# Fused block (GRU, state-space mixer, attention and experts): the 16-tap convolution of the mixer moved onto TensorE, with shifted copies made by transfers

## What is computed

```python
zxbcdt = x @ W_in                                   # x: the GRU's output, (32, 128, 128)
xBC = zxbcdt[..., D_INNER:D_INNER + CONV_DIM]       # 384 channels
kernel = conv_w.T[:, None, :]                       # conv_w: (384, 16)
xBC = jax.lax.conv_general_dilated(xBC, kernel, window_strides=(1,), padding=[(D_CONV - 1, 0)],
    dimension_numbers=('NWC', 'WIO', 'NWC'), feature_group_count=CONV_DIM) + conv_b
xBC = jax.nn.silu(xBC)
xs, Bm, Cm = ...                                    # 256, 64 and 64 channels of xBC
# scan over time: h = h * dA + dt * x * B;  y = h . C;  gated by silu(z), normalised, @ W_out
```

## Time and profile before

| | |
|---|---|
| median of 3 runs | 2272.22 us (2269.23 to 2278.43) |
| the profiled execution | 2269.55 us, its span 2267.7 us |
| busy share of the span | PE 89%, DVE 75%, ACT 44%, POOL 20% |
| chain that ended last | PE 47%, DVE 30%, ACT 9%, issue 8% |
| GRU and loads | 0 to 264.7 us |
| mixer with convolution | 264.7 to about 630 us |
| end of the mixer, then the later layers | to 2267.7 us |

### The profile page before, as it was taken

How to read it: one execution, slowest core, us unless ns; L and a number is a source line. 1 busy time by engine, 2 the same in 40 slices (tenths; PEclk the granted TensorE clock), 3 DMA queues, 4 the chain that set the end, 5 groups by cost and what they waited for, 6 DMA issues and landing times.

```text
span 2267.7 us, 62486 instructions
## 1 busy us (share of the span) xinstructions
PE 2011.8 (89%) x25711; PEld 1278.0 (56%) x25787; DVE 1698.1 (75%) x3792; ACT 1008.1 (44%) x2835; POOL 459.9 (20%) x794
## 2 busy tenths in 40 slices
PE   7888888998886898898799999985999789999998
PEld 5555534444453444343576677763666556677776
DVE  3443489999965888777888888844999668888887
ACT  2333245666553221221555555542544445555555
POOL 2211000000000434336012222243432111121200
PEclk8999699999978999999999999996999999999999
DMA  2000000000010000000311111106553211111111
GB/s 61 3 4 4 2 1 1 1 1 1 1 38 15 0 1 1 1 1 1 112 48 44 44 44 44 39 4 130 107 108 73 65 40 44 39 44 44 44 57 38
DMA packets 76038, 76.61 MB, mean 34 GB/s; under 512 B 15756, under 2 KB 57060, under 8 KB 74180
## 3 DMA queue, kind: packets, MB, share of 16 engines
q1 hardware_dynamic: 71848, 70.11, 12.3%
q10 hardware_dynamic: 3904, 2.49, 0.4%
HBM read 60.09 MB, written 11.82 MB: 32 GB/s over the span
## 4 chain that ended last, share of the span: by engine, by line
PE 47%; DVE 30%; ACT 9%; issue 8%; DMA 1%; POOL 1%; ACTq 1%; SPq 1%; another core or an unknown queue 1%; DVEq 0%; POOLq 0%
PE B L85 46%; DVE work L107 6%; DVE work L2117 4%; DVE hr L2081 3%; DVE work L2125 3%; ACT work L103 2%; ACT hr L103 2%; ACT ltc L103 2%; DVE work L1496 1%; ACT catt L103 1%; DVE gzh L107 1%; ACT ghh L103 1%; DVE work L1040 1%; ACTq L2404 1%; DVE grh L107 1%
## 5 line engine op out<-in xcount | busy, mean ns | idle before, releaser
L85 PE MATMUL B<-gr,wres 128*128 128x512 f32 x1248 | 354.5, 412 | 16.4 <-DVE work L2125 10.1
L103 ACT ACTIVATE work<-B 128x512 f32<-128x512 f32 (+7 forms) x468 | 240.1, 529 | 145.4 <-PE B L85 90.2
L2167 POOL COPY G<-lh 128x32 f32<-128x32 f32 x256 | 148.2, 579 | 680.0 <-DVE lh L107 680.0
L85 PE MATMUL B<-work 128*128 128x128 bf16 (+3 forms) x1408 | 260.3, 312 | 28.0 <-ACT work L103 7.0
L85 PEld LDWEIGHTS B<-gr,wres 128*128 128x128 f32 x1248 | 215.1, 189 | 83.7 <-DVE work L2125 27.4
L103 ACT ACTIVATE hr<-work 128x512 fp32r<-128x512 f32 x272 | 173.0, 636 | 147.0 <-DVE work L2125 77.5
L85 PEld LDWEIGHTS B<-work 128*128 128x128 bf16 (+2 forms) x1408 | 141.4, 127 | 139.1 <-issue 79.9
L2081 DVE TENSOR_TENSOR hr<-work,hr 128x512 fp32r<-128x512 f32 x272 | 186.5, 686 | 8.1 <-ACT hr L103 6.6
L2117 DVE TENSOR_TENSOR work<-work 128x512 f32<-128x512 f32 x256 | 178.9, 699 | 16.1 <-ACT work L103 8.9
L107 DVE SCALAR_TENSOR_TENSOR work<-work,cw 128x512 f32<-128x512 f32 x240 | 179.2, 747 | 5.9
L85 PE MATMUL B<-hr,wres 128*128 128x512 f32 x624 | 178.0, 394 | 1.0 <-DVE hr L2081 1.0
(11 more groups left out here) (262 smaller groups left out, 3777.8 us busy)
## 6 DMA issues: line engine op xcount, KB each, us to landing
work<-wdr SPq DMA_DIRECT2D x128, 256.0 KB, 3.1
scr<-catt SPq DMA_DIRECT2D x144, 64.0 KB, 2.8
work<-scr SPq DMA_DIRECT2D x16, 384.0 KB
work<-scr SPq DMA_DIRECT2D x16, 192.0 KB
catt<-in_L_ffn_ew SPq DMA_DIRECT2D x24, 128.0 KB, 2.2
work<-scr SPq DMA_DIRECT2D x16, 128.0 KB
out<-work SPq DMA_DIRECT2D x32, 64.0 KB, 2.2
work<-in_x ACTq DMA_DIRECT2D x2, 512.0 KB, 5.3
```

What stands on the lines that cost most here:

```text
L85: return e.matmul(out, lhsT, rhs, start=start, stop=stop, skip_group_check=True)
L103: return e.activation(out, in_, func, bias=bias, scale=scale)
L2167: e.tensor_copy(self.G[:, :, t], self.lh[:, t % 4, :]).then_inc(*inc("l.pool", "h", li, t))
```

## The change

All 16 taps go to PE. For that the 128 rows of the array no longer hold 128 channels, but 32 channels four times, each copy shifted by four more steps; the four column strips of the array (32 outputs each) take the four sets of 32 channels. In one wave, the four strips each do four taps for their 32 channels; four waves with the start moved by one column do all 16. A piece is so 4 waves of 4 matmuls of 32 x 512.

- The shifted copies are XR (two buffers in `spare`, which grows to 5120 columns): 4 row groups g, 4 sets of channels j. Each (g, j) is one transfer inside SBUF of 32 partitions x 4 x 131 words, from XP. SP issues these 16 transfers for each piece in the new `conv_sp` (L798), once `conv.x` of the piece is there and `conv.taps` of the piece two before has freed the buffer. PE waits for all 16 (`conv.r`).
- DVE's ten stt and `conv.acc` go. ACT's tanh waits for its own `conv.b`, and XP is freed by the transfers.
- The input product of piece n + 1 is now issued ahead of the taps of piece n, and the first one a turn before the loop; ACT's copy moves with it.
- The tap matrices (48 of 128 x 32 instead of 18 of 128 x 128) are made by three tensor_tensor on POOL after steps 60, 64 and 68 of the GRU, from the stacked identity `id32` (one reduce on DVE) and `cwp` (four more loads of 32 x 12 x 4 words on SP). DVE's 18 tensor_scalar go.

The diff, cut to its core:

```diff
-NT = 6
+NT = 16
...
-        for c in range(3):
-            for k in range(NT):
-                ts(e, self.tap[:, c * NT + k, :], self.ident[:], self.cw[:, c, k:k + 1], ALU.mult)
-                yield
+        red(e, self.id32[:], self.ident[:].rearrange("p (j m) -> p m j", j=4), ALU.add)
...
     def conv_pe(self, e):
+        e.wait_ge(*at("conv.tap"))
+        inputs(0)
+        yield
+        for n in range(24):
+            if n < 23:
+                inputs(n + 1)
+            yield
+            e.wait_ge(*at(f"conv.r{n % 2}", n))
+            if n:
+                e.wait_ge(*at("conv.b", n - 1))
+            for m in range(NT // 4):
+                for j in range(4):
+                    last = mm(e, BT[32 * j:32 * j + 32, :], self.tap[:, NT // 4 * (4 * (n % 3) + j) + m, :],
+                              self.XR[n % 2][:, 4 * j:4 * j + 4, m:m + 128], m == 0, m == NT // 4 - 1)
+                if m < 2:
+                    yield
+            last.then_inc(*inc("conv.taps", n))
+            yield
...
     def conv_dve(self, e):
-                e.wait_ge(*at("conv.b", n))
-                for k in range(NT, 16):
-                    stt(e, acc, X[:, :, 1 + k:129 + k], self.cw[:, c, k:k + 1], acc, ALU.mult, ALU.add)
...
+    def conv_sp(self, e):
+        for n in range(24):
+            e.wait_ge(*self.at("conv.x", n))
+            if n >= 2:
+                e.wait_ge(*self.at("conv.taps", n - 2))
+            for g in range(4):
+                for j in range(4):
+                    e.dma_start(self.XR[n % 2][32 * g:32 * g + 32, 4 * j:4 * j + 4, :],
+                                self.XP[n % 3][32 * j:32 * j + 32, :, 1 + NT // 4 * g:128 + NT // 4 * (g + 1)])
```

More of the change, by code:

```diff
@@ L171, in __init__ @@
         self.bank = [ctx.enter_context(nc.psum_tensor(f"B{i}", [128, 512], F32)) for i in range(8)]
-        with nc.sbuf_tensor("spare", [128, 3072], F32) as self.spare:
+        with nc.sbuf_tensor("spare", [128, 5120], F32) as self.spare:
             pass
@@ L255, in sync @@
         self.load_sp(e)
+        self.conv_sp(e)
         self.cprep_sp(e)
@@ L516, in gru_pool @@
                 next(rest, None)
+            if t in (60, 64, 68):
+                x = t - 60
+                e.wait_ge(*at("mprep.dve", "id32"))
+                e.tensor_tensor(self.tap[:, x * NT // 4:(x + 4) * NT // 4, :], bc(self.id32[:], 1, NT),
+                                bc(self.cwp[:, x:x + 4, :].rearrange("p x m -> p (x m)"), 2, 32), ALU.mult).then_inc(
+                    *inc("conv.tap"))
             yield
@@ L536, in lay_mamba @@
         self.h0T = sb("h0T", [64, 256])
-        self.tap = self.area([self.work, 74 * 256 - 3 * NT * 128], [128, 3 * NT, 128])
+        self.cwp = sb("cwp", [128, 12, NT // 4])
+        self.id32 = sb("id32", [128, 32])
+        self.tap = self.area([self.work, 74 * 256 - 96 * NT], [128, 3 * NT, 32])
+        w = [self.spare, 0]
+        self.XR = [self.area(w, [128, 16, 127 + NT // 4]) for _ in range(2)]
         w = [self.work, 0]
@@ L570, in mprep_load @@
             pairs.append((self.cb[:, c:c + 1], col(I["L0_attn_conv_b"][c * 128:c * 128 + 128])))
+        taps = I["L0_attn_conv_w"].rearrange("(x r) k -> r x k", r=32)
+        for g in range(4):
+            pairs.append((self.cwp[32 * g:32 * g + 32, :, :], taps[:, :, NT // 4 * g:NT // 4 * (g + 1)]))
         for d, s in pairs:
@@ L604, in mprep_dve @@
             yield
-        for c in range(3):
-            for k in range(NT):
-                if c + k == 0:
-                    e.wait_ge(*at("xt", 7))
-                ts(e, self.tap[:, c * NT + k, :], self.ident[:], self.cw[:, c, k:k + 1], ALU.mult)
-                yield
+        red(e, self.id32[:], self.ident[:].rearrange("p (j m) -> p m j", j=4), ALU.add).then_inc(*inc("mprep.dve", "id32"))
+        for _ in range(6):
+            yield
         e.wait_ge(*at("mprep.act", "A"))
@@ L672, in conv_pe, with inputs @@
         e.wait_ge(*at("mprep.dve", "A"))
[L673 to L680, removed]
-                yield
[L682 to L693, removed]
+        e.wait_ge(*at("conv.tap"))
+        def inputs(n):
+            if n:
+                e.wait_ge(*at("conv.x", n - 1))
+            mm(e, BI[:], self.win[:, 256 + n % 3 * 128:384 + n % 3 * 128], flat(self.G, UNITS[n // 3]), True, True).then_inc(
+                *inc("conv.in", n))
+        inputs(0)
[5 more added lines that the diff above has]
+            e.wait_ge(*at(f"conv.r{n % 2}", n))
+            if n:
+                e.wait_ge(*at("conv.b", n - 1))
[6 more added lines that the diff above has]
+            last.then_inc(*inc("conv.taps", n))
+            yield
+            if n % 3 == 2:
+                yield
     def conv_act(self, e):
@@ L707, in tanh @@
         def tanh(n):
-            e.wait_ge(*at("conv.acc", n))
+            e.wait_ge(*at("conv.b", n))
             if n >= 2:
@@ L712, in conv_act, with inputs @@
         e.wait_ge(*at("conv.pad"))
+        def inputs(n):
+            e.wait_ge(*at("conv.in", n))
+            if n >= 3:
+                e.wait_ge(*at(f"conv.r{(n - 3) % 2}", n - 3))
+            act(e, self.XP[n % 3][:, :, 16:144], BI[:].rearrange("p (b t) -> p b t", b=4), ACT.Copy).then_inc(
+                *inc("conv.x", n))
+        inputs(0)
+        yield
         n = 0
@@ L750, in silu @@
                 stt(e, cv[0:64, c, :], th[0:64, :], 1.0, cv[0:64, c, :], ALU.add, ALU.mult).then_inc(*inc("conv.silu", n))
-        for _ in range(4):
+        for _ in range(5):
             yield
@@ L755, in conv_dve @@
             for c in range(3):
-                X, acc = self.XP[n % 3], self.cvb[u % 4][:, c, :].rearrange("p (b t) -> p b t", b=4)
                 yield
@@ L759, in conv_dve @@
                     silu(n - 1)
-                e.wait_ge(*at("conv.b", n))
-                for k in range(NT, 16):
[L762 to L767, removed]
+                for _ in range(3):
+                    yield
                 n += 1
@@ L771, in conv_dve @@
         yield
+    def conv_sp(self, e):
[3 more added lines that the diff above has]
+                e.wait_ge(*self.at("conv.taps", n - 2))
+            else:
+                e.wait_ge(*self.at("conv.pad"))
+            for g in range(4):
+                for j in range(4):
+                    e.dma_start(self.XR[n % 2][32 * g:32 * g + 32, 4 * j:4 * j + 4, :],
+                                self.XP[n % 3][32 * j:32 * j + 32, :, 1 + NT // 4 * g:128 + NT // 4 * (g + 1)]).then_inc(*self.dma(f"conv.r{n % 2}", n))
     def conv_pool(self, e):
```

## The result

The changed kernel takes 2290.24 us (median of 5 runs, 2285.11 to 2293.76), the kernel before 2272.73 in the same comparison: a ratio of 1.0077, 95% interval 1.006 to 1.0093. It is slower by 0.8%, where 1.5% faster was forecast. The profiled execution took 2293.76 us with a span of 2292.0, against 2269.55 and 2267.7 before.

The account below looks back on a forecast made before the run. DVE (88.35 us busy) and PE (85.97) were both near full in a 94.80 us period, neither alone the bound. Running pattern -36 and start +3 on the profiled 2269.55, plus 2.7 for the median, gave 2239 us; range 2206 to 2290.

Parts of the forecast that it names:

- What the strips cost: PE's convolution taps: a wave of four strips about 0.86 us, 3.74 a piece instead of 5.17, saving 8.4 us a period.
- What a transfer costs: SP's transfers inside SBUF: 0.62 us each to issue, 2.2 to land, 12.2 us from copy to last landing.
- the rival of slow transfers: Convolution transfers at 0.95 us or more each set the pace: 2290 us, at 1.2 us each 2380; chance 0.12.
- What the transfers add to a period: Running pattern: late transfers show 0.65 us at four of six pieces, some 3 us a period, bounds 0 and 7.5.
- A period after, without transfers in the way: Running pattern of convolution and mixer: 94.8 less 8.4 (PE's strips) less 5.5 (DVE relieved), 80.9 us.
- little gained: Rival in the running pattern: transfer latency or ACT takes DVE's place, period 91 to 95, 2262 to 2280 us; chance 0.13.
- The start (+3): First pieces before the first cross: transfers pace them every 10 us, first cross near 313, 3 us later.
- POOL is idle, so its products are hidden: GRU: POOL's three tap products, 1.28 us each, fit its idle time and cost nothing; uncovered 4 us.
- DVE's tap builds (0): GRU: dropping DVE's 18 tap builds of 0.28 us gains nothing, as they were hidden before the next gate.
- Slower: Whole kernel slower by over 0.5%: chance 0.16, of which slow transfers 0.12, strips in a row 0.03, little gained 0.01.

Follow-up runs that it names:

- before_one_stt: The kernel before with one of ten convolution stt per piece on DVE (tap 15), taps 6 to 14 left out: 2244.01 us, ratio 0.9876.
- four_transfers: The changed kernel with 4 of the 16 transfers of each piece, other row groups of XR left zero: 2250.53 us, ratio 0.9904.
- two_ahead: The changed kernel with three XR buffers, input products and copies issued two pieces ahead instead of one: 2270.1 us, ratio 1.0003.
- late_two_queues: The changed kernel with the edits of late_products and two_ahead, and eight of each piece's sixteen transfers on POOL's queue: 2251.43 us, ratio 0.9911.
- before_products: The kernel before with POOL's three 128x512 products added after GRU steps 60, 64 and 68, written where nobody reads: 2280.07 us, ratio 1.0033.
- late_products: The changed kernel with POOL's three tap products after the GRU's last step instead of after steps 60, 64, 68: 2282.29 us, ratio 1.0047.
- late_two_split: The changed kernel with the edits of late_products and two_ahead, and four of eight decay tiles per sequence on DVE: 2261.74 us, ratio 0.9951.
- queues_split: late_two_queues with four of eight decay tiles per sequence moved from ACT to DVE: 2240.98 us, ratio 0.9848; run again 2239.52 us, ratio 0.9853.

## Why the prediction was wrong, point by point

- **What the strips cost: right, with 2 us too much of it counted.** 192 records were busy for 23.8 us a period, where 72 took 32.7: 8.9 less (8.4 forecast). Groups of 32 records take 3.64 to 3.66 us at full clock, so a wave of four strips with four different moving tiles takes 0.9 us. The time in which PE is busy with anything fell less, 6.1 us at clock 1.00 (83.4 in before_one_stt, 77.3 in four_transfers). Of the difference 0.5 us is in the `dg` products; where the rest lies was not found.
- **What a transfer costs: right.** 0.60 us to issue, 2.1 to land, 12.3 from copy to taps (0.62, 2.2 and 12.2 forecast). So the rival of slow transfers falls.
- **What the transfers add to a period: right in size** (3 forecast, 3.6 of waits; 4.4 by four_transfers), at one piece in six and not at four.
- **"A period after, without transfers in the way" (80.9 us): this step failed.** It took PE's 8.4 and DVE's 5.5 off the same period as if PE's other waits stayed as they were. four_transfers shows 87.7: PE's busy time fell by 7.4 us, but its idle time, 8.8 before, did not fall by 5.5; it was 9.2. Taps were also the cover under which ACT made the next decays: with 5.17 us of them a piece PE waited 0.3 us for decays, with 3.7 us 4.8 to 5.8, with 0.9 us 9.7 to 11.1. The last step is at the same order of the lists; in the first the sums were also moved between the waves, and how the 4.5 us divide between the two is not shown. The prediction noted ACT's busy time (58.5 us) and stopped there; "ACT takes the place of DVE" stood only under little gained, with 0.13, and that is what the pattern did. Moving half of the decays to DVE did not bring them back, since DVE's list then delays the next link.
- **The start (+3): failed, +14.** I let the copies follow one another every 10 us, the cadence of the transfers. But two pieces are ahead at most, and the third input product stands behind the taps of the first in PE's list: copy 2 came 25.7 us after copy 0 (271.23, 296.89), not 20, and copy 3 again behind the taps of piece 1. At the four pieces PE waited 10.2, 2.8, 6.5 and 4.3 us for transfers. The granted clock fell too, to 0.74 in the start: three of the four pieces took 5 to 6.2 us of strips in place of 3.65. four_transfers, two_ahead and late_two_queues each take part of it away.
- **"POOL is idle, so its products are hidden" (0, or 4 uncovered): failed, 6 to 8 us.** That is by the medians of before_products and late_products. In single profiles the first input product is 4.4 to 9.5 us later than before with the products in the GRU, and 1.5 us earlier to 1.8 later in the kernels with strips that have them behind it; the 9.5 of two_ahead holds a dip of the clock at 50 to 90 us (0.76 and 0.68) that no product stands beside. Idle time of the engine was the wrong row to read; the question was whom it disturbs while it works. DVE's 0.19 us stt took 1.03 us beside it. The Trainium skill (SBUF — State Buffer, "SBUF: two separate sides") says that DVE and GpSimd share a port pair as an exclusive lock, held for a whole instruction, also by a DVE operation with two inputs in SBUF against a GpSimd operation that reads SBUF. The row agrees: the stt ends where POOL's product ends. With the rule in mind the forecast would have been some 3 us for the waits (an estimate: three products of 1.05 us); the clock's fall after them was not to be had from it.
- **DVE's tap builds (0): not measured by themselves.** late_products has its first input product 1.1 us earlier than before, but other kernels without the builds and without POOL's products in the GRU have it up to 1.8 us later.
- **The rest of the 17.5 us is partly open.** The end of the mixer cost 4.3 us after state product 26. There the three profiles of kernels with stt take 119.5 to 119.8 us, the nine with strips in four waves 120.3 to 126.3, whether their transfers are hidden or not. It goes with the granted clock: the three longest, 124.9 us or more, are at 0.74 to 0.80, the four shortest with strips at 0.81 to 0.83. What makes the clock differ there was not tested. The 7.5 us in layers whose code did not change belong to this one execution: the medians differ by 17.5, not 24.3.
- **The chances.** Slower had 0.16, mostly by slow transfers; that rival's 2290 us met the time by luck, since a transfer cost what was forecast. All three failed steps erred in one direction: each was costed by what its own engine can do, and not by what stands around it in the lists.

## What to carry to other kernels

When work in an in-order list gets shorter, look at what the instruction behind it waits for: that wait may have been covered by the work removed, and it comes back. Here, with DVE relieved, 4.9 us less work on PE shortened the period by 0.6 us, and a further 15.7 us by 8.9. A chain of transfers is priced by latency, not by cadence, wherever the next producer's instruction stands behind the consumer's in some list; fetching two pieces ahead and dividing issues over two queues was worth some 30 us here. And an idle engine is free only if it shares nothing with the busy one.

## What the chip showed that I had not expected

- A POOL product of 1.05 us with two inputs in SBUF stretches a DVE stt from 0.19 to 1.03 us; three of them in the recurrence cost 6 to 8 us. In the profile of before_products two thirds of 7.1 us go with the granted clock, which was 0.60 over 20 us behind pauses of PE of 1 us.
- Four column strips with four different moving tiles overlap almost fully: 3.64 to 3.66 us for 32 records of 512 columns (16 products) in the starts of late_two_split, late_two_queues and queues_split, where 16 at the 0.86 us of a full-width tap would be 13.8 us. By these records four strips reach about 3.8 times. The Trainium skill (TensorE: Matmul & The Clock Gate, "Measured speedup vs the span model") has 2.38 for three; no row here has three of them by themselves apart from the earlier trace rows, which gives 2.6.
- POOL issues a transfer of 32 x 4 x 131 elements in 0.55 us, SP in 0.60; side by side their landings took 2.7 and 2.9 us.
